# A graph network's edge passes: TensorE signals once in a round, products follow the first edge layer by two rounds and sums by five

## What is computed

```python
e = relu(edge_weight1 @ W_l0 + b_l0) @ W_l1 + b_l1        # of each edge
def gine(x, src, dst, e, W1, b1, W2, b2):
    agg = segment_sum(relu(x[src] + e), dst)
    return relu(relu((x + agg) @ W1 + b1) @ W2 + b2)
h = relu(gine(x, ..., W00, b00, W01, b01))
h = relu(gine(h, ..., W10, b10, W11, b11))
x = layernorm(x + h)
edge_feat = mlp(edge_attr_4)                              # product, relu, batch norm over all edges
message   = mlp(concat(x[src], x[dst], edge_feat))        # the same, 288 -> 96
x = layernorm(x + segment_sum(message, dst) + mlp(x))
```

## Time and profile before

| | us |
|---|---|
| three executions | 18908.68, 18910.0, 18912.41 (median 18910.0) |
| the profiled execution | 18918.55 |
| its span, first to last instruction | 18916.7 |

### The profile page before, as it was taken

One profiled execution on the slowest core, in us unless ns is written; L12 is line 12 of the kernel. 1 busy time (PEld: TensorE's weight loads), 2 busy tenths in 40 slices (PEclk: granted clock), 3 DMA queues, 4 the chain that ended last, 5 costly groups with the idle time before them and its releaser, 6 DMA issues. The chain is left out here.

```text
span 18916.7 us, 156984 instructions
## 1 busy us (share of the span) xinstructions
PE 9564.5 (51%) x34170; PEld 6800.3 (36%) x34170; DVE 7554.3 (40%) x15601; ACT 4986.1 (26%) x11066; POOL 9163.3 (48%) x9682
## 2 busy tenths in 40 slices
PE   3445455455455455555555555554444444444445
PEld 2333333333333333333333333333333333333334
DVE  3333333333333333333333333334444444544445
ACT  1222222222222222222222222223333232323323
POOL 5555554454454544444444444444544444454543
PEclk9999999999999555555555555555555555555555
DMA  2111111111111111111111111111111111111111
GB/s 67 31 32 31 33 32 32 32 32 32 31 33 39 34 33 33 33 34 34 34 34 34 34 34 34 34 32 33 34 34 35 34 34 34 33 34 33 35 34 34
DMA packets 580725, 646.62 MB, mean 34 GB/s; under 512 B 411208, under 2 KB 411689, under 8 KB 579722
## 3 DMA queue, kind: packets, MB, share of 16 engines
q0 software_dynamic: 309504, 476.02, 12.0%
q1 hardware_dynamic: 219142, 139.69, 2.9%
q10 hardware_dynamic: 51712, 27.54, 0.5%
HBM read 604.68 MB, written 39.43 MB: 34 GB/s over the span
## 5 line engine op out<-in xcount | busy, mean ns | idle before, releaser
L1271 PE MATMUL ps_pre<-w_e,conv_hid 97*128 97x96 f32 x12896 | 3277.5, 434 | 2812.9 <-issue 1418.0
L1271 PEld LDWEIGHTS ps_pre<-w_e,conv_hid 97*128 97x128 f32 x12896 | 2879.0, 327 | 3554.5 <-issue 3304.7
L1271 PE MATMUL ps_pre<-last_w_q,last_hid 128*128 128x96 f32 x6448 | 1626.0, 432 | 2105.3 <-issue 997.0
L534 PE MATMUL ps_hid<-conv_row,w_hid 12*96 12x512 bf16 x1736 | 1087.3, 626 | 2824.5 <-issue 1809.5
L263 POOL DMA_INDIRECT early_got<-h_rows,early_idx x1612 | 1524.1, 945 | 1779.0 <-DVE ps_pre L632 1196.6
L1271 PEld LDWEIGHTS ps_pre<-last_w_q,last_hid 128*128 128x128 f32 x6448 | 1440.0, 327 | 2495.3 <-issue 2244.5
L263 POOL DMA_INDIRECT conv_got<-h_rows,early_idx x1612 | 1524.2, 946 | 1651.5 <-DVE ps_pre L632 1187.8
L263 POOL DMA_INDIRECT early_got<-p_rows,early_idx x1612 | 1524.3, 946 | 1555.9 <-DVE ps_pre L632 1070.0
L263 POOL DMA_INDIRECT last_got<-p_rows,early_idx x1612 | 1524.2, 946 | 1536.9 <-DVE ps_pre L632 1063.8
L263 POOL DMA_INDIRECT conv_got<-in_x_rows,early_idx x1612 | 1524.0, 945 | 1463.0 <-DVE ps_pre L632 977.2
L263 POOL DMA_INDIRECT early_got<-in_x_rows,early_idx x1612 | 1528.0, 948 | 1453.0 <-DVE ps_pre L632 979.1
(11 more groups left out here) (255 smaller groups left out, 11988.8 us busy)
## 6 DMA issues: line engine op xcount, KB each, us to landing
conv_row<-ea_parts SPq DMA_DIRECT2D x372, 84.5 KB
last_row<-ea_parts SPq DMA_DIRECT2D x372, 84.5 KB
early_got<-in_x_rows,early_idx POOLq DMA_INDIRECT x1612
conv_got<-in_x_rows,early_idx POOLq DMA_INDIRECT x1612
early_got<-h_rows,early_idx POOLq DMA_INDIRECT x1612
conv_got<-h_rows,early_idx POOLq DMA_INDIRECT x1612
early_got<-p_rows,early_idx POOLq DMA_INDIRECT x1612
last_got<-p_rows,early_idx POOLq DMA_INDIRECT x1612
```

The source lines that it names most:

```text
L534: pe.matmul(ps["hid"][0][0:HC, 0:nt * P], w_hid[:], row[r][AT:AT + K, t0 * P:(t0 + nt) * P], start=True, stop=True).then_inc(s["hid"], 1)
L1271: mm = pe.matmul(ps["pre"][q % 2][:, t * C:(t + 1) * C], hid[q % 2][0:P if last else C1, t * P:(t + 1) * P], w_q[j % U][:, c * C:(c + 1) * ...
```

## The change

PE signals once in a round, on one new semaphore `round`, raised by the last product of `pre` (in the first two rounds by `hidden` or `features`, in the last ones by `segment` or the turn). Every engine that waited for `hid`, `f`, `pre`, `seg` or `turned` waits for a count of `round` instead, and so do SP and the waits of the node stages on PE (class `Rounds`). `hidden` gets a second bank. To make room, the row of node numbers is copied into free columns of the `pre` banks, and `own` is left to the last pass. `pre` follows `hidden` by two rounds (`AHEAD`), `segment` by five (`SUMS`), fold and turn by six. There are four one-hot buffers instead of two, and one feature buffer instead of two. On DVE and ACT, all steps of a chunk from the one-hot to the third part now stand in one round. The node stages stand three rounds later. In the last pass SP reads the seven row numbers in one go. The branch for other inputs, which is not taken here, is adapted.

```diff
+AHEAD = 2
+SUMS = AHEAD + 3
+FOLDS = SUMS + 1
...
+class Rounds:
...
+    def wait(self, eng, name, i):
+        if self.by_round:
+            eng.wait_ge(self.rounds, i * self.step + self.first + self.places[name] + 1)
...
-                hot = [sb(f"{name}_hot{i}", [P, CH * P], BF16, st) for i in range(2)]
+                hots = sb(f"{name}_hot", [P, NB * CH * W], BF16, st)
+                hot = [hots[:, i * CH * W:(i + 1) * CH * W] for i in range(NB)]
...
-                    feat = [sb(f"{name}_feat{i}", [C, CH * P], F32, st) for i in range(2)]
+                    feat = sb(f"{name}_feat", [C, CH * P], F32, st)
...
-                ps = pools(st, hid=1, pre=2, win=2, own=1, **(dict(feat=1, node=1) if stats else dict(f=1, tot=1) if last else dict(node=1, e=1)))
+                ps = pools(st, hid=2, pre=2, win=2, **(dict(feat=1, node=1) if stats else dict(own=1, f=1) if last else dict(node=1, e=1)))
...
-                def relu_hidden(act, q, b, n, free):
+                def relu_hidden(act, q, b):
                     nt = CHUNKS[q % NC_][1]
-                    act.wait_ge(s["hid"], n + 1)
-                    need(act, s["pre"], free)
-                    act.activation(hid[b][0:C, 0:nt * P], ps["hid"][0][0:C, 0:nt * P], ACT.Relu).then_inc(s["rhid"], 1)
...
+                    act.activation(hid[b][0:C, 0:nt * P], ps["hid"][b][0:C, 0:nt * P], ACT.Relu).then_inc(s["rhid"], 1)
...
-                    need(act, s["seg"], part_free)
...
                     def free(lag, k, j):
 
                         if not opening(k) or j >= U:
-                            sp.wait_ge(s[sem], Q * k + NC_ * (j - U + 1))
+                            sp.wait_ge(s["round"], Q * k + NC_ * (j - U + 1) + lag)
...
-                            features(pe, r, q, q % 2, Q * k + q, left(k, q))
+                            mm = features(pe, r, q, Q * k + q)
+                        if opening(k) and q < AHEAD:
+                            mm.then_inc(s["round"], 1)
...
-                        mm.then_inc(s["pre"], 1)
+                        mm.then_inc(s["round"], 1)
...
-                            mm = sum_tile(pe, ps["win"][r], hot[q % 2], q, t, t0 + t == 0, t0 + t == T - 1)
-                        mm.then_inc(s["seg"], 1)
+                            mm = sum_tile(pe, ps["win"][r], q, t, t0 + t == 0, t0 + t == T - 1)
...
-                    staged(pe, ITERS, Q, [(0, hidden_rows), (1, pre), (4, turn_window), (3, segment)],
+                    staged(pe, ITERS, Q, [(SUMS, segment), (0, hidden_rows), (FOLDS, turn_window), (AHEAD, pre)],
...
+                    def hidden_cols(k, q):
+                        act.wait_ge(s["round"], Q * k + q + 1)
+                        relu_hidden(act, q, q % 2)
+                        if stats:
+                            relu_features(act, q, Q * k + q)
...
-                    plan += [(2, lambda k, q: second_part(act, q, q % 2, Q * k + q)), (1, message)]
+                    plan = [(0, hidden_cols), (AHEAD, message), (AHEAD, lambda k, q: second_part(act, q, q % 2, Q * k + q))]
...
                     def one_hot(k, q):
                         j, _, t0, nt = chunk(q)
-                        need(v, s["seg"], left(k, q))
+                        v.wait_ge(s["round"], rounds(k, q + AHEAD))
...
-                    plan = [(3, lambda k, q: third_part(v, q, q % 2, Q * k + q)),
-                            (4, fold_window), (2, one_hot)]
+                    plan = [(0, near_rows)] if last else []
+                    plan += [(AHEAD, one_hot), (AHEAD, add_rows), (SUMS, fold_window),
+                             (AHEAD, lambda k, q: subtract_first(v, q, q % 2, Q * k + q))]
+                    if stats:
+                        plan += [(0, lambda k, q: batch_statistics(v, k * V + chunk(q)[0], q, Q * k + q))]
+                    plan += [(AHEAD, lambda k, q: third_part(v, q, q % 2, Q * k + q)), (FOLDS, add_window)]
```

More of the change, by code:

```diff
@@ L92, in phases, with __init__, of @@
                 body(k, late)
+class Rounds:
+    def __init__(self, sem, rounds, step, first, places):
+        self.sem, self.rounds, self.step, self.first, self.places = sem, rounds, step, first, places
+        self.names, self.by_round = tuple(places), True
+    def of(self, ins):
+        if not self.by_round:
+            ins.then_inc(self.sem, 1)
+    def wait(self, eng, name, i):
+        if self.by_round:
+            eng.wait_ge(self.rounds, i * self.step + self.first + self.places[name] + 1)
+        else:
+            eng.wait_ge(self.sem, len(self.names) * i + self.names.index(name) + 1)
 class Marks:
@@ L133, in staged @@
     phases(eng, iters, iters if start is None else start, body)
-    for place, stage in side:
-        if place >= half and start < iters:
-            stage((iters - start) * parts - 1)
-    for q in range(max(lag for lag, _ in plan)):
+    rounds = max(lag for lag, _ in plan)
+    for q in range(max([rounds, *(place - half + 1 for place, _ in side)])):
+        for place, stage in side:
+            if place == half + q and start < iters:
+                stage((iters - start) * parts - 1)
         for lag, stage in plan:
@@ L490, in edge_pass @@
                     cuts = [(x[:, 0:min(wide, COLS - c * wide)], slice(c * wide, min((c + 1) * wide, COLS)))
-                            for c, x in enumerate([*ps["hid"], *ps["pre"], *ps["win"], *ps["node"], *ps["own"]][:pieces])]
+                            for c, x in enumerate([*ps["hid"], *ps["pre"], *ps["win"], *ps["node"]][:pieces])]
                     assert len(cuts) == pieces and D * PIECE <= 512
-                iota = ps["own"][0][:, CH * C:CH * C + P]
-                squares = ps["own"][0][:, 0:CH * C]
+                iota = [x[:, CH * C:CH * C + P] for x in ((ps["own"] * 2) if last else ps["pre"])]
+                squares = ps["own"][0][:, 0:CH * C] if last else None
+                totals = ps["f"][0][:, C:3 * C] if last else None
                 turned = [x[:, 512 - W:512] for x in ps["win"]]
@@ L526, in edge_pass, with hidden @@
                 w_hid = w_hid1 if last else w_hid0_at if stats else w_hid0
-                def hidden(pe, r, q, n):
+                def hidden(pe, r, q, b, free):
                     t0, nt = CHUNKS[q % NC_]
-                    need(pe, s["rhid"], n)
+                    need(pe, s["rhid"], free)
                     if last:
-                        need(pe, s["hot_t"], n)
-                    pe.matmul(ps["hid"][0][0:HC, 0:nt * P], w_hid[:], row[r][AT:AT + K, t0 * P:(t0 + nt) * P],
-                              start=True, stop=True).then_inc(s["hid"], 1)
@@ L537, in features @@
-                def features(pe, r, q, b, n, free):
+                        need(pe, s["hot_t"], free)
+                    return pe.matmul(ps["hid"][b][0:HC, 0:nt * P], w_hid[:], row[r][AT:AT + K, t0 * P:(t0 + nt) * P],
+                                     start=True, stop=True)
+                def features(pe, r, q, n):
                     t0, nt = CHUNKS[q % NC_]
                     need(pe, s["rf"], n)
-                    pe.matmul(ps["feat"][0][0:C, 0:nt * P], w_hid1[0:KE, 0:C], srow[r][:, t0 * P:(t0 + nt) * P],
-                              start=True, stop=True).then_inc(s["f"], 1)
@@ L642, in prepare @@
                     if not split_edges:
-                        v.tensor_copy(iota, node_row[:])
+                        for x in iota[:1 if last else 2]:
+                            v.tensor_copy(x, node_row[:])
                     for i in range(2):
@@ L1255, in hidden_rows @@
                             pe.wait_ge(s[f"row{r}"], ROWS * (turn(k, j) + 1))
-                        hidden(pe, r, q, Q * k + q)
+                        mm = hidden(pe, r, q, q % 2, left(k, q))
                         if stats:
@@ L1336, in add_window @@
                         r = j % U
-                        v.wait_ge(s["turned"], k * V + j + 1)
+                        v.wait_ge(s["round"], rounds(k, q + FOLDS))
                         need(v, s[f"win{1 - r}"], turn(k, j) + r)
@@ L1435, in body @@
                             n = k * NC_ + c
[L1436 removed]
+                            hidden(pe, 0, c, 0, n).then_inc(s["hid"], 1)
                             if stats:
[L1438 removed]
+                                features(pe, 0, c, n).then_inc(s["f"], 1)
                             pe.wait_ge(s["rhid"], n + 1)
@@ L1567, in _ @@
                         pe.wait_ge(s["t_in"], 1)
-                        pe.matmul(ps["tot"][0][:, 0:2 * C], ones[:], tot[:], start=True, stop=True).then_inc(s["t_pe"], 1)
+                        pe.matmul(totals, ones[:], tot[:], start=True, stop=True).then_inc(s["t_pe"], 1)
                     pe.wait_ge(s["init"], 1)
```

122 lines of the change are left out of this document (63 added, 59 removed).

## The result

The changed kernel takes 19,184.5 us (median of four, 19,168.7 to 19,206.9) against 18,909.3 us (four, 18,906.4 to 18,912.4): ratio 1.0146, 95% interval 1.0129 to 1.0164, +275 us. The forecast was 19,250.

What follows compares the result with a forecast made beforehand. Bound taken: PE executes at once, but its news arrives late and in order while the gathers run. (−0.5 + 0.8 + 2.4) × 124 = +335, +10 for the ends, on 18,910 gives about 19,250 us; range 18,300 to 20,050.

Steps and rivals of the forecast that it cites:

- Fewer signals: 0 taken: PE's signals, 9,052 cut to 2,604: no gain taken; bounds nothing to 258 us of gain.
- the rival that made signals the cost: Each late hop costs some 5 us per signal, so one signal a round gives some 15,300 us; chance 0.17.
- the small fixed price: Each PE signal costs a small fixed price: −258 us and the chains hidden, about 18,650 us; chance 0.04.
- The price per matmul, some 2 us: PE's news during the gathers is delayed mainly per matmul record, some 2 us each, and little per signal.
- The extra round in the stretch: Second hidden bank lets PE fit three product rounds instead of two into the gathers' stretch, saving 3.7 us in first pass.
- First pass, −0.5 forecast: First pass, a slab: −3.7 us for a saved quiet round, +3.2 for steps in a row; bounds −1.6 and +0.5.
- Second pass, +0.8 forecast: Second pass, a slab: like the first, but the single feature buffer costs part of the extra round; bounds −0.3 and +4.0.
- Last pass, +2.4 forecast: Last pass, a slab: DVE's serial steps cost +3.6 us over four quiet rounds, distance returns 1.2; bounds −1.0 and +4.5.
- the sign: Expected in last pass's profile: DVE idle about 0.4 and 0.5 us between addition, subtraction and third part; quiet round 4.8 us.
- SP, the one-hot and part buffers, the ends: SP's single read and the dropped buffer wait: 0 each; sums draining three rounds more at pass ends: +10 us.
- The chain that hides: Distance pays and the last pass's chain hides: all three lower bounds hold, −360 us, about 18,550; chance 0.19.
- lost whole rounds: Coarse signal costs whole rounds, as PE runs with no distance in the second pass: +1,080 us, about 19,990; chance 0.13.

Runs made afterwards that it cites:

- late case's run with four gathers: Changed kernel, last pass's steps ordered as before, 4 gathers a slab instead of 26 after each pass's first iteration: 11,187 us where the kernel before took 19,006.
- late case: Chip or condition of the prediction and its result: kernel before 18,909 us, changed kernel 19,184.5; met again in the last series, kernel before 19,006.
- prompt case: Chip or condition of all other series of experiments: kernel before 12,270 to 12,296 us; changed kernel 12,631.4 against 12,296.2, ratio 1.0274.
- 14,136 more: Changed kernel with 14,136 more signals that nobody waits for: 12,616.4 us; with 4 gathers a slab, 11,526.8 against 11,527.5 us without them.
- The runs for it: Four one-column products ahead of each hidden product: changed kernel 12,614.6 us; with the last pass's steps as before 12,281.9 against 12,273.0, ratio 1.0008.
- The uncovered run: Changed kernel with 4 gathers a slab instead of 26 after each pass's first iteration: 11,527 us, against 10,586 for the kernel before with the same edit.
- the run with a signal of its own: Changed kernel with the second pass's feature product raising its own signal again, for ACT's features' relu: 12,615.4 us, second pass 4,084 us as without it.
- in its old order: Changed kernel, last pass's DVE and ACT steps ordered as before, near rows and hidden relu one round later: 12,300.2 against 12,296.2 us for the kernel before, ratio 1.0003.

## Why the prediction was right, and where it was not

**The bound.** The reading that PE executes at once and that its news arrives late during the gathers holds in the changed kernel (22.6 us late), and the late case's run with four gathers ties the lateness to the gathers. It rests on the ends of matmuls as the profile puts them; whether PE is done at that moment no run tests. What it lacked: that the lateness is a condition of one chip or moment. The same program shows none of it elsewhere and takes a third less time. Nothing in the trace of before could tell.

**Fewer signals: 0 taken.** Right. In the late case the result itself speaks: with one signal a round instead of three or four the news is as late as before, and the total is nowhere near the 15,300 us of the rival that made signals the cost. In the prompt case 14,136 more cost nothing, so there the small fixed price is out as well; in the late case it wasn't tested.

**The price per matmul, some 2 us.** The runs for it met the prompt case, but the traces speak against it. It was read from three hops of the earlier trace rows; the next ones of the same stretch are

```profile
7545.65 0.66 PE L534 MATMUL ps_hid<-conv_row,w_hid 12*96 12x512 bf16 x1 [3.48 <-issue]
...
7562.89 0.95 POOL L263 DMA_INDIRECT conv_got<-h_rows,early_idx  x1 [0.30 <-issue]
...
7567.40 0.59 ACT L547 ACTIVATE conv_hid<-ps_hid 96x512 f32<-96x512 f32 x1 [11.79 <-DMA dst_n<-in_dst_n]
...
7569.35 0.55 DVE L632 TENSOR_TENSOR ps_pre<-ps_pre,conv_got 128x384 f32<-128x384 f32 x1
```

The gather of 7562.89 is the last of the burst. Between the hidden product of 7545.65 and the end of the product of 7555.84 lie nine records, 18 us at that price, and their news is at most 7569.35 − 7567.40 = 1.95 us apart. In the last pass of the changed kernel two products whose news is late end 3.7 us apart, with 13 records between them, and the two relus that wait for them start 4.2 us apart (median of 125 such pairs), not 26. What does fit is the end of the burst: in the kernel before, 235 additions of the first and last passes start over 12 us behind their product, and 229 of them follow the last gather so far by more than 3 us, most by 5.2 to 5.5 from its start. Why the news then comes is open. The term of 0 for the signals doesn't hang on this price; its reason does.

**The extra round in the stretch.** It is there: product rounds that start between 7 us after the first and 2 us after the last gather of a burst went from 1.6 to 2.4, 1.3 to 1.5 and 2.0 to 3.0 a slab, by a count over both traces. What it saves is another matter.

**First pass, −0.5 forecast, +0.2 measured.** Within its bounds. The extra round came in 0.8 of the slabs, but the count by additions above shows no quiet round saved, 4.99 instead of 5.05: the product runs within the stretch, and its addition still comes behind it. The quiet rounds are 0.7 us a slab longer in all and the late part is 0.5 shorter. So neither −3.7 nor +3.2 is seen at its size; they were set against each other, and their difference came out small. The uncovered run has +0.5 without any late news.

**Second pass, +0.8 forecast, −1.0 measured.** This step failed, and the value lies outside its bounds of −0.3 and +4.0. The one feature buffer is waited for, as said (22.14 us), but it was charged as an addition, 1.3 us a slab. I read it as a stop that takes the place of another that would have ended as late. The late part of a slab is 1.1 us shorter (29.5 against 30.6). How much that wait still costs is open, since the run with a signal of its own met the prompt case.

**Last pass, +2.4 forecast, +2.9 measured.** The place and the mechanism are shown: 4.94 us a round where the sum said 4.8, with idle pieces at the two hand-overs (0.94 and 0.55 us; the sign gave 0.4 and 0.5, though the sum's own 1.48 less the addition makes 0.9), and the loss goes when the order goes. The terms were mis-sized in opposite directions. The sum had four quiet rounds at +0.9 and gave back 1.2; in fact a slab has 5.85 rounds at 5.23 us instead of 5.03 at 3.92, +10.9, and the shorter wait gives back 8.1. The error of each is larger than the effect; the total was right in good part by luck, because they cancel. The 1.2 given back had no row behind it.

**SP, the one-hot and part buffers, the ends.** Nothing of them is seen in the prompt case: the first two passes are 3,976 and 4,084 against 3,976 and 4,078 us, and the last, in its old order, 4,097 against 4,097.

**The rivals.** The chain that hides did not come, nor did lost whole rounds.

## What to carry to other kernels

Signals that nobody waits for cost nothing here, but merging them isn't free: each waiter now waits for the last thing that the signal covers, and an order of steps that relied on the earlier signal becomes a ring. On an engine with over 90% in the stretch that counts, keep steps of different chunks in one round, so that hand-overs to another engine fall behind other work. A loss can be hidden by whatever bound lies above it (7 us a slab uncovered, 2.7 under the gathers), so an edit should be timed once without that cover. A price read from a few hops should be held against the next ones in the same rows.

## What was not expected of the hardware

The same program took 18,909 us on one chip and 12,270 to 12,296 us on others, with busy times within 1% of each other. In the late case a completion of PE reaches ACT and DVE over 20 us late while POOL's indirect gathers run (22.6 in the timeline above), and within 0.04 us in the quiet part; SP's issue of one row transfer of the second pass (L520) took 0.70 us in the median against 0.32 in the prompt case. With 4 gathers a slab instead of 26 the late case costs nothing behind the first iteration. What makes a chip late was not found.
